# A decoder layer on one core: cross-attention's keys and values are projected during self-attention, on TensorE right behind the scores

## The reference

```python
x = layernorm(x + self_attention(x))            # 32 heads of 16, causal, ALiBi bias, biases on qkv and out
x = layernorm(x + cross_attention(x, context))  # 32 query heads of 128, 8 key/value heads of 128, RoPE on q and k
x = layernorm(x + feed_forward(x))              # relu^2 MLP 512-1024-512, latent experts, top-2 routing, layer norm
```

## Time and profile before

| | |
|---|---|
| median of three runs | 1057.08 us |
| span of the profiled execution (all four stages) | 1065.3 us |
| PE busy in it | 987.9 us, 93% |
| PEld / DVE / ACT / POOL busy | 825.1 / 765.2 / 503.1 / 437.0 us |
| DMA moved | 52.02 MB, mean 49 GB/s |
| stage A, B, C, D, about | 0 to 86, to 277, to 926, to 1065 us |

### The profile page before, as it was taken

How to read it: one execution, slowest core, us unless ns; L and a number is a source line. 1 busy time by engine, 2 the same in 40 slices (tenths; PEclk the granted TensorE clock), 3 DMA queues, 4 the chain that set the end, 5 groups by cost and what they waited for, 6 DMA issues and landing times. The chain is left out here.

```text
span 1065.3 us, 17470 instructions
## 1 busy us (share of the span) xinstructions
PE 987.9 (93%) x4940; PEld 825.1 (77%) x4940; DVE 765.2 (72%) x2345; ACT 503.1 (47%) x1581; POOL 437.0 (41%) x367
## 2 busy tenths in 40 slices
PE   6997999999778999999999999999999999789996
PEld 5875999999556887887887887787778777578885
DVE  4445568888697787777877877777777788784646
ACT  4325669898335435445345435444444435441220
POOL 1762000000357556546546646637546455340101
PEclk9997579999899999999999999999999999999998
DMA  8032212222221102002002002002001002210001
GB/s 298 1 99 60 60 37 59 46 58 70 87 82 50 40 11 65 31 5 69 30 0 76 22 0 79 20 0 79 20 15 64 10 18 73 78 62 10 30 1 39
DMA packets 41372, 52.02 MB, mean 49 GB/s; under 512 B 5104, under 2 KB 21616, under 8 KB 41200
## 3 DMA queue, kind: packets, MB, share of 16 engines
q1 hardware_dynamic: 41008, 50.44, 15.6%
q0 software_dynamic: 320, 1.05, 0.3%
HBM read 40.98 MB, written 2.10 MB: 40 GB/s over the span
## 5 line engine op out<-in xcount | busy, mean ns | idle before, releaser
L1060 POOL TENSOR_TENSOR C_t<-C_t 128x512 f32<-128x512 f32 x80 | 104.5, 1310 | 153.2 <-DVE C_t L965 153.2
L817 ACT ACTIVATE C_prob<-C_prob,C_ntop 128x128 f32<-128x128 f32 x256 | 99.8, 391 | 87.9 <-DVE C_ntop L997 87.8
L34 PE MATMUL C_yb<-C_woh,C_oh 128*128 128x512 f32 x256 | 107.5, 420 | 17.4 <-POOL C_wol L1088 12.3
L774 ACT ACTIVATE C_qh<-C_t 128x512 fp32r<-128x512 f32 x64 | 40.5, 633 | 141.0 <-POOL C_t L1060 141.0
L1010 DVE TENSOR_TENSOR C_ol<-C_ov,C_oh 128x512 fp32r<-128x512 f32 x64 | 44.2, 691 | 85.8 <-ACT C_oh L792 85.8
L34 PE MATMUL C_pj<-xTh,wh 128*128 128x512 f32 x256 | 101.3, 396 | 3.7 <-DVE xTl L128 2.2
L492 ACT ACTIVATE B_prob<-B_prob,B_ntop 128x128 f32<-128x128 f32 x256 | 99.2, 392 | 8.5 <-DVE B_ntop L573 7.3
L34 PE MATMUL C_yb<-C_woh,C_ol 128*128 128x512 f32 x256 | 102.8, 402 | 0.0
L34 PE MATMUL C_yb<-C_wol,C_oh 128*128 128x512 f32 x256 | 102.6, 401 | 0.0
L34 PE MATMUL C_pj<-xTh,wl 128*128 128x512 f32 x256 | 100.8, 394 | 0.0
L34 PE MATMUL C_pj<-xTl,wh 128*128 128x512 f32 x256 | 100.6, 393 | 0.0
(11 more groups left out here) (219 smaller groups left out, 2867.1 us busy)
## 6 DMA issues: line engine op xcount, KB each, us to landing
stage<-wq_dram SPq DMA_DIRECT2D x32, 256.0 KB, 3.4
stage<-wo_dram SPq DMA_DIRECT2D x32, 256.0 KB, 3.1
qs<-q SPq DMA_DIRECT2D x16, 256.0 KB, 2.7
kd<-k SPq DMA_DIRECT2D x128, 32.0 KB, 2.0
stage<-wqkvT_dram SPq DMA_DIRECT2D x10, 256.0 KB, 5.9
x<-x_nat_dram SPq DMA_DIRECT2D x1, 2048.0 KB, 10.1
stage<-wk_dram SPq DMA_DIRECT2D x8, 256.0 KB, 3.2
stage<-ctxT_dram SPq DMA_DIRECT2D x8, 256.0 KB, 3.0
```

The source lines that it names most:

```text
L34: mm = eng.matmul(out, stationary[i], moving[j], start=first and n == 0, stop=last and n == len(PASSES) - 1)
L817: last = eng.activation(e, e, ACT.Exp, bias=ntop[:, s % 2, h:h + 1], scale=1.0, accum_out=total[:, s % 2, h:h + 1])
L1060: eng.tensor_tensor(t1[:, j % 2, :], t1[:, j % 2, :], t2[:, j % 2, :], ALU.add).then_inc(s_sum, 1)
```

## The change

- Scores of self-attention: q and k no longer stay on chip. Stage A stores their high and low parts in DRAM, and per batch 16 DMAs bring them back stacked (`SelfHeads`), so that one matmul of 256 columns does all three passes of two heads, and the ALiBi bias as well. The DVE maximum then adds one causal tile for all heads.
- Keys and values of cross-attention are projected in B: 16 key tiles and 16 value tiles of 12 matmuls, half a tile (six matmuls) in each of the steps 2 to 65, on TensorE right behind the scores of the step. Tile j of the keys is on TensorE in steps 4j+2 and 4j+3, its cosine product on DVE in 4j+4, its sine products at the end of 4j+5, its sum on POOL in 4j+5 and its high and low parts in 4j+6. Tile j of the values is on TensorE in 4j+4 and 4j+5. The projections have two PSUM banks, one for the keys and one for the values. The results go to DRAM.
- The context's split moves from the start of C to the end of A. The transposes of the probabilities have one PSUM bank in B where they had two, and two in C where they had one.
- C projects query tiles alone: one per step, four before the first step and a fifth in front of it. On DVE the rotation stands behind the reciprocal. Keys and values come by one DMA of 2 MB per group; the weights `wo` have two buffers. Value transposes and their copies are gone.
- B and C are written out in full, without a loop.

```diff
+class SelfHeads:
...
+        pairs, tok = slice(self.PAIRS * i, self.PAIRS * (i + 1)), slice(b * S, (b + 1) * S)
+        both = lambda d, s: d[pairs, s, :, :, tok].rearrange("j t d n -> (t d) j n")
+        high = lambda d, s: d[pairs, s, 0, :, tok].rearrange("j d n -> d j n")
+        for s in range(2):
+            r, cols = 3 * DH * s, slice(s * S, (s + 1) * S)
+            for dst, src in ((self.q[i][r:r + 2 * DH, :, :], both(self.q_d, s)),
+                             (self.q[i][r + 2 * DH:r + 3 * DH, :, :], high(self.q_d, s)),
+                             (self.k[i][r:r + DH, :, cols], high(self.k_d, s)),
+                             (self.k[i][r + DH:r + 3 * DH, :, cols], both(self.k_d, s))):
+                eng.dma_start(dst.bitcast(F32), src).then_inc(self.s_load[i], 16)
...
+SELF_PIECES = (("k", 0, 0), ("v", 0, 0), ("v", 1, 0), ("v", 2, 1), ("v", 3, 1), ("o", 0, 2), ("o", 1, 4), ("o", 2, 6),
+               ("k", 1, 8), ("o", 3, 10), ("v", 4, 12), ("v", 5, 14), ("k", 2, 16), ("v", 6, 18), ("v", 7, 20),
+               ("k", 3, 24), ("k", 4, 32), ("k", 5, 40), ("k", 6, 48), ("k", 7, 56))
...
+        def keys(n, lag):
+            f = n - OFF - 2 - lag
+            return f // 4 if f % 4 == 0 and 0 <= f < 2 * TILES else None
+        def values(n, lag):
+            f = n - OFF - 4 - lag
+            return f // 4 if f % 4 == 0 and 0 <= f < 2 * TILES else None
...
+            def project(f, part):
+                i, out = f // 2, pj[f % 2][:, :]
+                if part == 0 and f % 2 == 0:
+                    eng.wait_ge(ring.s_lo, PIECE["k", i // 2] + 1)
+                    wait(eng, s_sin, i)
+                elif part == 0:
+                    eng.wait_ge(ring.s_lo, PIECE["v", i // B * C + C - 1] + 1)
+                    wait(eng, s_vlo, i)
+                for c in range(2 * part, 2 * part + 2):
+                    if f % 2 == 0:
+                        st = [t[:, c * P:(c + 1) * P] for t in wk]
+                        mv = [t[:, c, i % 2 * HALF:(i % 2 + 1) * HALF] for t in cT]
+                    else:
+                        st = [t[:, c, i % B * S:(i % B + 1) * S] for t in cT]
+                        mv = [t[:, i // B, c, :] for t in wv]
+                    mm = product(eng, out, st, mv, c == 0, c == C - 1)
+                if part == 1:
+                    mm.then_inc(s_pj, 1)
...
-                        eng.wait_ge(s_load[G // PAIR], LOADS * (b + 1))
+                        heads.loaded(eng, b, G // PAIR)
                     wait(eng, s_top, n - 1)
-                    c, cols = G // 2, slice(4 * (G % 2), 4 * (G % 2) + 4)
-                    product(eng, sc[G % 2][:, :].rearrange("p (h s) -> p h s", h=HG), [qs[:, 2 * c + j, :] for j in range(2)],
-                            [kd[:, 2 * c + j, cols, :] for j in range(2)], True, True).then_inc(s_sc, 1)
+                    for i in range(2):
+                        j = 2 * (G % PAIR) + i
+                        mm = eng.matmul(sc[G % 2][:, 2 * S * i:2 * S * (i + 1)], heads.q[G // PAIR][:, j, :],
+                                        heads.k[G // PAIR][:, j, :], start=True, stop=True)
+                    mm.then_inc(s_sc, 1)
+                if 0 <= n - OFF < 2 * TILES:
+                    project((n - OFF) // 2, (n - OFF) % 2)
...
-                    wait(eng, s_phi, m - 1)
-                    wait(eng, s_plo, m - 1)
+                    wait(eng, s_phi, m)
+                    wait(eng, s_plo, m)
...
+                cos, sin = (trig[:, 2 + i, :].unsqueeze(1).broadcast_to([P, 4, S]) for i in range(2))
+                j = keys(n, 0)
+                if j is not None:
+                    eng.wait_ge(s_pj, 2 * j + 1)
+                    wait(eng, s_klo, j)
+                    eng.tensor_tensor(by_batch(t1[:, :]), by_batch(pj[0][:, :]), cos, ALU.mult).then_inc(s_cos, 1)
+                j = keys(n, 1)
+                if j is not None:
+                    eng.tensor_tensor(by_batch(t2[0:64, :]), by_batch(pj[0][64:128, :]), sin[0:64], ALU.mult)
+                    eng.tensor_tensor(by_batch(t2[64:128, :]), by_batch(pj[0][0:64, :]), sin[64:128],
+                                      ALU.mult).then_inc(s_sin, 1)
+                j = values(n, 0)
+                if j is not None:
+                    eng.wait_ge(s_vhi, j + 1)
+                    eng.tensor_tensor(v_out[:, :, 1, :], by_batch(pj[1][:, :]), v_out[:, :, 0, :].bitcast(F32),
+                                      ALU.subtract).then_inc(s_vlo, 1)
...
+            def project(r):
...
+                eng.wait_ge(ring.s_lo, 2 * Q * g + j + 1)
+                wait(eng, s_sin, r - 1)
...
+                if n + PRE < TILES:
+                    rotate(n + PRE)
```

More of the change, by code:

```diff
@@ L220, in project_self @@
     at = {p: n for n, p in enumerate(pieces)}
-    tiles = [("qk", m, h) for h, part in ((0, 0), (0, 1), (1, 0), (1, 1)) for m in range(part * C, part * C + C)] + \
+    order = [("qk", m, h) for h, part in ((0, 0), (0, 1), (1, 0), (1, 1)) for m in range(part * C, part * C + C)] + \
             [("v", b, 0) for b in range(B)]
-    order = tiles
+    QK = heads.TILES
     Q_DONE = 3 * C
@@ L369, in _ @@
                 if kind == "qk":
-                    t = q if m < C else k
-                    hi, lo = (t[:, 2 * (m % C) + j, h * HALF:(h + 1) * HALF] for j in range(2))
+                    hi, lo = (heads.tiles[i % heads.RING][:, j, :] for j in range(2))
                 else:
@@ L494, in step @@
                     last.then_inc(s_exp, 1)
-                if isinstance(b, int) and (b, G) in SPLIT:
-                    c = SPLIT.index((b, G))
-                    eng.wait_ge(s_wst, 16 * (c + 1))
-                    eng.activation(wout[0][:, c, :], wst[:, :], ACT.Copy).then_inc(s_whi, 1)
+                j = keys(n, 2)
+                if j is not None:
+                    eng.wait_ge(s_sum, j + 1)
+                    wait(eng, s_kout, 16 * j)
+                    eng.activation(k_out[:, :, 0, :], by_batch(t1[:, :]), ACT.Copy).then_inc(s_khi, 1)
+                for i in splits(n):
+                    kind, j, _ = SELF_PIECES[i]
+                    if kind == "k":
+                        wait(eng, s_pj, 4 * j - 1)
+                    ring.hi(eng, i, target(i)[0])
             loop(eng, step)
@@ L705, in attend_cross @@
-        SPLITS = {2: [("wo", h) for h in range(Q)] + [("w", 0)], 3: [("w", 1), ("w", 2)],
-                  4: [("w", 3)], 5: [("w", K)], 6: [("w", V)]}
-        def splits(g, s):
-            return [x for x in SPLITS.get(s, ()) if not isinstance(g, int) or g < G - 1 or (g == G - 1 and x[0] == "wo")]
-        def slot(what):
-            kind, j = what
-            return (FIRST + (j if kind == "wo" else Q + j)) % RING
-        def next_pieces(g, s):
-            first = 2 * (B * g + s - NS + 4) if isinstance(g, int) else -1
+            for n in range(NS + 4):
+                step(n)
@@ L755, in _ @@
-            cycle(0)
-            with eng.Fori(1, G - 1) as g:
-                cycle(g)
-            cycle(G - 1, last=True)
-            eng.wait_ge(s_wlo, TILES * G)
-            for i in range(2):
-                eng.wait_ge(s_wolo[i], 2 * G)
+            for i in range(ring.SLOTS, len(sources)):
+                ring.load(eng, i, sources[i])
+                if i == 2 * Q - 1:
+                    load_kv(1)
+                if i >= 22 and (i - 22) % B == 0:
+                    load_kv((i - 22) // B + 2)
@@ L1130, in feed_forward @@
         tile_of = lambda kind, j: [weights.place(kind, j, lo) for lo in range(2)]
-        wdown = pair("down", [P, M, D])
+        wdown = weights.wide[1]
         wlat = [[t[:, j, :] for t in w] for j in (5, weights.BASE["exp"])]
```

791 lines of the change are left out of this document (385 added, 406 removed).

## The result

The changed kernel took 1145.53 us, the median of four runs (1141.92 to 1160.17), against 1058.76 us before in the same series: 1.079 times the time, 95% interval 1.074 to 1.084. The forecast was 1101 us (1035 to 1130): right in sign, 44 us too fast. The execution of 1160.17 us had a lower mean clock of TensorE (0.908 against 0.922 to 0.925) and is left out of the ratio. The profiled execution has a span of 1143.3 us.

The account below looks back on a forecast made before the run. Self-attention was taken as bound by TensorE, cross-attention by TensorE with a DVE and ACT ring about as long. Span 1065.3 + 79 + 24 - 57 - 2 = 1109 us, less 8: 1101 us, range 1035 to 1130.

Parts of the forecast that it names:

- The work of a step in B: Self-attention: TensorE has 2.93 us per step for scores, half a tile, values' product and transposes; 1.9 before.
- `yb` 2.7: Self-attention: the output projection on TensorE adds 2.7 us once per batch, 19 us for seven.
- The 5.5 us from the first scores to the first key tile: Start of self-attention: 5.5 us until the first weight is split, behind the first exponentials.
- The new wait: Self-attention: TensorE stands still 2.8 us once in four steps until DVE's sine products free the keys' bank; 15 times.
- The clock: Self-attention: TensorE's clock falls behind each of 15 waits, 1.6 us each, +24 us; bounds from 0.
- The drain of B: End of self-attention: draining the last work takes 12 us.
- In front of B: Before self-attention: 4 us for the last head load, issued behind ring loads; bounds 0 and 10.
- stage A: First stage: its first 80 us keep their work, context's splits run under the value tiles; 0, bounds -3 and +5.
- -57 and -2: Cross-attention: sixty steps fall from 9.55 to 8.6 us, -57 us; four rotations instead of five at its start, -2.
- Rival 1: Cross-attention: `ntop` comes ahead of POOL's low part, turn 7.55 us, 60 us less, 1041 us; chance 0.17.
- Transfers in B: Self-attention: data transfers were given no term in the sum.

Follow-up runs that it names:

- the two runs that shortened or covered its chain: Each one edit to the changed kernel: sine products one step earlier, 1090.26 us; half tile last in TensorE's step, 1095.40 us.
- the filled wait: Changed kernel plus ten extra 512-column matmuls on TensorE between scores and key tile in the steps with the stall: 1108.62 us, ratio 1.039.
- fewer loads: Changed kernel with only 20 pieces, not 24, loaded ahead of the 32 head stores in stage A: 1146.79 us, ratio 1.081.
- heads first: Changed kernel with the second load of the first batch's heads issued ahead of the four weight loads: 1144.66 us, ratio 1.079.
- low part behind `ntop`: Changed kernel with POOL's low part of a rotated tile waiting for the step's `ntop` in cross-attention: 1103.41 us, ratio 1.037.

## Why the prediction was right in sign and wrong in size

- *The work of a step in B*, 2.93 us: 2.95 measured. Right. `yb` 2.7: 2.88. The 5.5 us from the first scores to the first key tile: 107.4 to 112.9, right.
- *The new wait*, 15 times 2.8 us, 42 in all: 15 times, 38.7 us in all. Right, and the two runs that shortened or covered its chain left 3.1 and 1.2 us of it.
- *The clock*, 15 falls at 1.6 us: here the term was mis-sized. That there would be a fall for each wait was nearly so (14 of 15); it costs 2.5 us on average, 37 us by the filled wait, where I had 24. The 1.6 came from one fall of less than 4 us; another in the same trace, behind a wait of 1.99 us before 303.31, I had not read (matmuls 0.43 apart from 304.5 to 307.5). It is as short, but here the low level held from 241.4 to 248.3, and for about 6.8 us or more behind nine of the fourteen.
- *The drain of B*, 12 us: 23.9, from the first tile behind the last step's transposes, at 396.5, to the first transposes of C at 420.4. It was 18.3 before (259.9 to 278.2) and was to be read from the trace, so the 12 was too small for the old drain already. The last output projection runs at 1.2 GHz (0.43 between matmuls) in both. New are two half tiles, 2.7 us at full clock, and a longer wait for the output's last part on DVE, 4.0 us where it was 1.4.
- *In front of B*, 4 us (0 to 10) and *stage A*, 0 (-3 to +5): together +21.4. This is the step that failed outright. The forecast said that the first 80 us of A keep their work and has no term for the stores of the heads: it put them at nothing without a reason. They are 512 KB per tile, which land every 2.57 us, about TensorE's own pace, they began late, and ACT's copies stand behind them: TensorE waits 3.6 us at 42.7, and without the late begin A's last matmul comes 8.6 us earlier. From 44 to 60 us the share of the DMA engines was 0.53, and SP was issuing these stores one behind the other, 1.2 us each (median); which of the two sets the 2.57 us stays open. The context's splits share DVE and POOL with the values' tiles, and the last heads' load ends the stage. The Trainium skill, SBUF — State Buffer, section Who interferes with whom, says that a VectorE instruction with two SBUF inputs contends with a GpSimd instruction that reads SBUF; the trace agrees (1.33 against 0.69 us).
- *C*: -57 and -2, measured -65. The mechanism was right to 0.1 us: step 8.47 for 8.5 to 8.6, `ntop` 1.10 for 1.11. The two terms were not, and the sum is near by luck in part: from the first to the last `ntop` C took 522.9 us where it took 591.7, 69 less, since with 8.47 for the 8.6 and a few steps below it there was more to gain, and to its first `ntop` it took 40.3 us where it took 36.4, 4 more and not 2 less. Rival 1 missed by 0.2 us of POOL's lead. With POOL's low part put behind `ntop` the step is 7.53, as it said (7.55), and C is 52 us shorter, where it had 60.
- *Transfers in B*: the forecast has no term for them. In the changed kernel that held, but only because the new waits hid them; the values' store decided as soon as these were gone.

The misses: 17.4 in A, 12 in the drain, about 13 in the clock, -6 in C, and -2 elsewhere are the 34 us of span between 1109 and 1143. The measured time lies outside the range of 1035 to 1130: A and the time in front of B together came out above their bounds (15 at most, 21.4 measured), the drain had none, and the clock's 37 lay above the 24 of the sum, all on the same side. I had treated two readings I did not make (the stores, the drain) and one taken from a single fall (its length) as small.

## What to carry to other kernels

Place work on an in-order engine by the latest thing that it needs, not by what it follows: the same six matmuls cost 50 us more ahead of the work that covers the release of their bank than behind it, and only about 7 more once the bank was freed a step earlier. Count a wait of TensorE like these (2.2 us and more) twice, once as itself and once as the slow stretch behind it: here 39 us and 37 us. Read from more than one fall how long that stretch lasts. When a wait is removed, look at what was late behind it (here a store issued behind eight loads), and where an instruction on one engine meets another's by 0.2 us, order the two by a semaphore.

## What the runs showed of the hardware that I had not expected

- The clock's price varies between executions of the same instructions: B took 313.0, 314.5, 318.5 and 327.3 us in four profiled runs (the changed kernel, fewer loads, heads first, low part behind `ntop`) whose B is alike in its instructions and in its waits at the keys' bank (38.7 to 38.8 us), with mean clocks of 0.83, 0.82, 0.81 and 0.78.
- The waits cost no clock when TensorE worked in them, even at useless matmuls: 0.84 (124 to 396) became 1.00 (124 to 358), in the run with the wait filled.
